# First stage of a graph and expert kernel: two node chunks with each edge group, eight places of edge coefficients, PSUM of the radial weights released at its last read

## The reference

```python
edge_index = jnp.stack([src, dst])
x = x + _L0_gnn_ref(_layernorm(x, axis=-1), edge_attr_3, edge_attr_8, L0_gnn_fc_w1, ...)

def _L0_gnn_ref(node_features, edge_vectors, edge_lengths_embedding, fc_w1, fc_w2, lin_w0, lin_w1, edge_index):
    sender, receiver = (edge_index[0], edge_index[1])
    ...
    sh1 = jnp.sqrt(3.0) * edge_vectors / (r + 1e-09)
    h = jax.nn.silu(edge_lengths_embedding @ fc_w1 / np.sqrt(NB))
    w = (h @ fc_w2 / np.sqrt(NH)).reshape(-1, NPATH, MUL)
    s = node_features[:, :MUL][sender]
    v = node_features[:, MUL:].reshape(-1, MUL, 3)[sender]
    dot = jnp.einsum('eui,ei->eu', v, sh1)
    crs = jnp.cross(v, sh1[:, None, :])
    m0 = (w[:, 0] * s + w[:, 3] * dot * inv_sqrt3) * inv_sqrt2
    m1 = (w[:, 1] * s * sh1 + w[:, 2] * v + w[:, 4] * crs * inv_sqrt2) * inv_sqrt3
    agg0 = jax.ops.segment_sum(m0, receiver, num_segments=NN) / AVG_NEIGH
    ...
    out0 = agg0 @ lin_w0 / np.sqrt(MUL)
    ...
    return upd + node_features
```

## Time and profile before

| | us |
|---|---|
| median of 3 runs | 1482.0 |
| profiled execution | 1486.56 |
| its span | 1484.8 |
| first stage, to the loads of the next | 389.4 |
| busy in the first 372 us: VectorE, GpSimd, ScalarE, TensorE | 314.0, 276.7, 273.3, 243.7 |
| mean granted TensorE clock in the first 372 us | 0.84 |

### The profile page before, as it was taken

The page is one execution under the profiler, slowest core; times in us unless marked ns, Lnnn a source line. Parts: engine busy times, 40 slices in busy tenths (PEclk is TensorE's granted clock), DMA queues, the critical chain, the costliest instruction groups (busy, mean ns, idle before and its releaser), DMA issues.

```text
span 1484.8 us, 26582 instructions
## 1 busy us (share of the span) xinstructions
PE 1223.6 (82%) x7872; PEld 1081.4 (73%) x7872; DVE 1015.4 (68%) x2130; ACT 932.9 (63%) x2049; POOL 1009.8 (68%) x915
## 2 busy tenths in 40 slices
PE   2335598998489523799999999999999999999993
PEld 0223365555355322799999999999999999999993
DVE  7889969996389897565755755665755575556653
ACT  4788967874257500666766766766766576667762
POOL 6886777875457302576777777777777777778785
PEclk9966788988799756899999999999999999999997
DMA  9999845543676101242433433343522343233333
GB/s 322 294 336 318 260 89 73 74 66 43 143 267 217 57 9 36 72 103 43 100 57 48 107 46 46 48 102 47 113 47 43 47 107 49 44 47 54 54 50 43
DMA packets 131625, 152.97 MB, mean 103 GB/s; under 512 B 17034, under 2 KB 118474, under 8 KB 131422
## 3 DMA queue, kind: packets, MB, share of 16 engines
q0 software_dynamic: 51456, 64.07, 27.4%
q1 hardware_dynamic: 58446, 66.59, 13.8%
q10 hardware_dynamic: 21648, 21.45, 4.2%
HBM read 98.79 MB, written 53.28 MB: 102 GB/s over the span
## 4 chain that ended last, share of the span: by engine, by line
PE 51%; issue 4%; POOL 2%; ACT 2%; DMA 1%; DVE 0%; ACTq 0%; POOLq 0%; DVEq 0%
PE f_ps_y L1533 25%; PE f_ps_h L1521 24%; PE f_ps_x L1511 2%; POOL out L1412 1%; POOL xg L1394 1%; POOL sg L1398 1%; ACT h_all L1461 0%; ACT h_hi L1460 0%; ACT f_xn L1445 0%; DMA sg<-stat_rows,idx_row 0%; DMA sg<-stat_rows,idx_now 0%; ACT y_all L1471 0%; DMA out<-clean,put_now 0%; ACT w_hi L1288 0%; DVE clean L1598 0%
## 5 line engine op out<-in xcount | busy, mean ns | idle before, releaser
L1460 ACT ACTIVATE h_hi<-f_ps_h,c_b 128x384 fp32r<-128x384 f32 (+1 forms) x416 | 237.0, 570 | 263.3 <-PE f_ps_h L1521 263.3
L1571 DVE TENSOR_TENSOR h_lo<-h_all,h_hi 128x768 fp32r<-128x768 f32 (+1 forms) x208 | 184.4, 886 | 257.5 <-ACT h_all L1461 257.1
L1533 PE MATMUL f_ps_y<-w_hi,h_hi 128*128 128x256 f32 x1136 | 325.1, 286 | 0.7 <-DVE h_lo L1571 0.7
L1533 PE MATMUL f_ps_y<-w_lo,h_hi 128*128 128x256 f32 x1136 | 319.8, 282 | 0.0
L1533 PE MATMUL f_ps_y<-w_hi,h_lo 128*128 128x256 f32 x1136 | 319.6, 281 | 0.0
L1412 POOL DMA_INDIRECT out<-clean,put_now x159 | 260.6, 1639 | 57.5 <-issue 49.3
L1394 POOL DMA_INDIRECT xg<-out,idx_now x159 | 193.1, 1214 | 130.8 <-issue 120.6
L1521 PE MATMUL f_ps_h<-x_hi,w_hi 128*128 128x384 f32 (+1 forms) x832 | 271.9, 327 | 7.9 <-issue 3.5
L1521 PE MATMUL f_ps_h<-x_lo,w_hi 128*128 128x384 f32 (+1 forms) x832 | 269.3, 324 | 0.0
L1521 PE MATMUL f_ps_h<-x_hi,w_lo 128*128 128x384 f32 (+1 forms) x832 | 269.0, 323 | 0.0
L1461 ACT ACTIVATE h_all<-f_ps_h,c_b 128x384 f32<-128x384 f32 (+1 forms) x416 | 237.9, 572 | 0.0
(11 more groups left out here) (214 smaller groups left out, 2285.9 us busy)
## 6 DMA issues: line engine op xcount, KB each, us to landing
shared<-out SPq DMA_DIRECT2D x40, 512.0 KB, 4.0
w_raw<-in_w SPq DMA_DIRECT2D x16, 1024.0 KB, 5.3
xin<-in_x SPq DMA_DIRECT2D x24, 512.0 KB, 8.0
out<-xin ACTq DMA_DIRECT2D x24, 512.0 KB, 7.2
shared<-in_x SPq DMA_DIRECT2D x16, 512.0 KB, 6.5
out<-shared ACTq DMA_DIRECT2D x16, 512.0 KB, 6.1
dst_row<-in_dst SPq DMA_DIRECT2D x20, 256.0 KB, 3.7
xg<-out,idx_now POOLq DMA_INDIRECT x159
```

The source lines that it names most:

```text
L1460: nc.scalar.activation(h_hi[:, f, :n * P], ps_h[:, f % SLOTS, :n * P], ACT.Relu, bias=b1[:, e, f:f + 1])
L1533: ins = nc.tensor.matmul(ps_y[:, i], x[:, f, i * P:(i + 1) * P], weights[s][:, w], start=i != 1 and f == 0 and n == 0, stop=f == KF - 1 an ...
L1571: tt(h_lo[:, pair, :n * P], h_all[j % 2][:, :, :n * P], h_hi[:, pair, :n * P].bitcast(F32), ALU.subtract).then_inc(h_lo_ready, 1)
```

## The change

Steps with two chunks: `STEPS` goes from 5 to 10, and each of VectorE's steps 0 to 7 has two chunks, one inside the messages and one behind them. Chunk coefficients are taken behind the messages. Edge statistics and coefficients have eight places (`AHEAD = 8`) and are spread by two small functions. On ScalarE the hidden layer of group g+1 comes ahead of its rows, the aggregate's copy between the two halves of the directions. On GpSimd each pair of gathers stands ahead of a batch's scales, with one or two edge scales behind; one batch fewer is done there (`BY_POOL` 7); the late gathers stand behind scatters 5, 6 and 7, edge scales seven groups ahead from scatter 3 on. SP loads the receivers' rows inside the loop over chunks. In the messages the last product that reads `ps_w` comes earlier and has a semaphore of its own, `w_taken`, on which TensorE's next radial weights wait. The line numbers of the changed kernel are a few higher up to the middle of the stage and lower after it (L402 becomes L399, L481 L479, L604 L601, L717 L715).

```diff
-    STEPS = 5
+    STEPS = 10
+    AHEAD = 8
-    BY_POOL = 8
-    assert NC == 4 * STEPS
+    BY_POOL = 7
+    assert NC == 2 * STEPS
...
-        edge_mv = [sb(f"edge_mv{h}", [P, GT, 2]) for h in range(4)]
+        edge_mv = [sb(f"edge_mv{h}", [P, GT, 2]) for h in range(AHEAD)]
...
@@ SP
-                if c % 4 == 1:
-                    next_embedding(c // 4)
-                    if c > 4:
-                        next_receivers(c // 4 - 1)
+                if c % 2:
+                    next_embedding(c // 2)
+                    if c > 2:
+                        next_receivers(c // 2 - 1)
...
@@ GpSimd
             for n in range(3, BY_POOL):
+                gather(2 * n - 1)
+                gather(2 * n)
                 node_scales(n)
-                for g in (2 * n - 1, 2 * n):
-                    if g < SLOTS:
-                        gather(g)
-                if n % 2:
-                    edge_scales(n // 2 + 2)
+                edge_scales(2 * n - 3)
+                if 2 * n - 2 < STEPS:
+                    edge_scales(2 * n - 2)
+            gather(2 * BY_POOL - 1)
             pool.wait_ge(chunks_known, 16)
             for g in range(EG):
                 scatter(g)
-                if STEPS <= g + 4 < EG - 1:
-                    edge_scales(g + 5)
-                if 1 <= g < 4:
-                    gather(SLOTS + 2 * g - 2)
-                    gather(SLOTS + 2 * g - 1)
+                if STEPS <= g + 7 < EG:
+                    edge_scales(g + 7)
+                if 5 <= g < 8:
+                    gather(SLOTS + 2 * (g - 5))
+                    gather(SLOTS + 2 * (g - 5) + 1)
...
@@ ScalarE
             for g in range(1, STEPS):
-                c = 4 * g
-                add_own_rows(c)
-                take_agg(g - 1)
-                radial_hidden(g + 1)
-                next_rows(g + 1)
-                add_own_rows(c + 1)
-                rows_by_direction(g + 1, (0, 1))
-                take_upd(g - 1)
-                add_own_rows(c + 2)
-                rows_by_direction(g + 1, (2, 3))
-                add_own_rows(c + 3)
-            store_rows(NC - 1, 1)
+                add_own_rows(2 * g)
+                radial_hidden(g + 1)
+                if g + 1 == STEPS:
+                    add_own_rows(2 * g + 1)
+                    store_rows(NC - 1, 1)
+                next_rows(g + 1)
+                rows_by_direction(g + 1, (0, 1))
+                take_agg(g - 1)
+                if g + 1 < STEPS:
+                    add_own_rows(2 * g + 1)
+                rows_by_direction(g + 1, (2, 3))
+                take_upd(g - 1)
             for g in range(STEPS, EG + 1):
                 if g + 1 < EG:
+                    radial_hidden(g + 1)
                     next_rows(g + 1)
-                    rows_by_direction(g + 1, range(GT))
+                    rows_by_direction(g + 1, (0, 1))
                 take_agg(g - 1)
                 if g + 1 < EG:
-                    radial_hidden(g + 1)
+                    rows_by_direction(g + 1, (2, 3))
                 take_upd(g - 1)
...
@@ TensorE, radial_second
-                    pe.wait_ge(msg_ready, g)
+                    pe.wait_ge(w_taken, g)
...
@@ VectorE
                 chain.mark(tt(tmp_d[:], tmp_f[:], w(3), ALU.mult))
+                chain.wait(1)
+                tt(vec(tmp_h), vec(tmp_a), w3(4), ALU.mult).then_inc(w_taken, 1)
                 chain.mark(tt(tmp_g[:], tmp_b[:], tmp_c[:], ALU.add))
-                chain.wait(2)
-                chain.mark(tt(vec(tmp_h), vec(tmp_a), w3(4), ALU.mult))
...
             def step(g):
                 receivers(g)
-                if g + 1 < STEPS:
-                    node_coefs(BATCH[4 * g + 2])
-                    node_statistics(4 * g + 4)
-                    messages(g, 4 * g + 5)
-                    edge_statistics(g + 3)
-                    node_coefs(BATCH[4 * g + 4])
-                    edge_coefs(g + 2)
-                    node_statistics(4 * g + 6)
-                    node_statistics(4 * g + 7)
+                if g + 2 < STEPS:
+                    messages(g, 2 * g + 4)
+                    node_coefs(BATCH[2 * g + 2])
+                    node_statistics(2 * g + 5)
                 else:
-                    if g + 1 == STEPS:
+                    if g + 2 == STEPS:
                         node_coefs(BATCH[NC - 1])
                     messages(g)
-                    edge_statistics(g + 3)
-                    edge_coefs(g + 2)
+                for n in range(EG):
+                    if statistics_step(n) == g:
+                        edge_statistics(n)
+                for n in range(EG):
+                    if coefs_step(n) == g:
+                        edge_coefs(n)
+            def statistics_step(n):
+                return (n - 3) // 2 if n < STEPS else n - 6
+            def coefs_step(n):
+                if n < 2:
+                    return -1
+                return (n - 1) // 2 if n < STEPS else n - 2
```

More of the change, by code:

```diff
@@ L264, in edge_and_node_block @@
         msg_ready = sem("msg_ready")
+        w_taken = sem("w_taken")
         row_ready = sem("row_ready")
@@ L322, in _ @@
             for c in range(NC):
-                for a in range(2):
-                    if 1 <= c and c + RING - 1 < NC:
+                if c:
+                    for a in range(2):
                         sp.wait_ge(x1_out[(c - 1) % RING][a], 16 * ((c - 1) // RING + 1))
-                        load_rows(c + RING - 1, a)
-                if 1 <= c and c + RING - 1 < NC:
+                        if c + RING - 1 < NC:
+                            load_rows(c + RING - 1, a)
                     sp.sem_inc(stored, 1)
```

42 lines of the change are left out of this document (18 added, 24 removed).

## The result

The changed kernel takes 1546.7 us (median of 4 runs, 1543.3 to 1552.5) against 1482.5 for the kernel before on the same chip: ratio 1.044, 95% interval 1.040 to 1.048. It is 64 us slower. The forecast was 1477.0 with a range of 1469 to 1489, and none of the rivals is near it. The profiled execution took 1543.27 us with a span of 1541.5, 56.7 more than before. The first stage accounts for that: the start of its last group of scatters, S(19), goes from 379.97 to 437.96, +58.0 us.

The account below looks back on a forecast made before the run. GpSimd's chain of scatters was taken to bound the first stage, with VectorE nearly as long. Start 127.4 plus intervals of 60.0, 64.5, 90.5 and 32.6 put S(19) at 375.0, -5.0 us: 1477.0 us, range 1469 to 1489.

Parts of the forecast that it names:

- what is late next: Steps with chunks: hidden layer waits for TensorE's aggregate, delaying the receivers' row; 1 to 2 us lost a step.
- the rest of the new order: Remaining reordering, with VectorE's leftover waits and extra 2.5 us: hidden by 24 us of slack, so no cost.
- the last eleven intervals: Last scatter intervals on GpSimd: eight of 11.31 us, then three of 10.86 with VectorE done; 123.1 us.
- S(0): Start of the first group's first scatter on GpSimd: 127.4, 3.0 us late; bounds 126.5 and 130.4.
- VectorE in the chunk steps: Steps 0 to 2 on VectorE, with two chunks each: 20.15 us a step.
- Waits for the receivers' row: VectorE's new wait: 2 us a step up to step 3, some 6 us more in steps 4 and 5.
- Five intervals beside traffic: First five scatter intervals, beside the chunks' transfers: 12.0 us each, 60.0 in all; ends 11.31 and 14.35.
- rival A: First five scatter intervals: beside chunk traffic each stays at 14.35 us, +6.8 us, 1489; chance 0.20.
- Three intervals with gathers: Scatters 5, 6 and 7 on GpSimd, eight gathers behind each: 21.5 us an interval, 64.5 in all.
- VectorE's wait for the weights goes: VectorE's waits for radial weights in PSUM fall from 18.0 us to under 3 through earlier release and hidden layer.
- The bound: First stage's end: set by GpSimd's chain of scatters at 375.0; VectorE's 336 and its 15.0 us path give 351.
- The falsifier written down: End of the first stage: argument wrong if last scatters wait for ScalarE's update, or S(19) comes before 360.

Follow-up runs that it names:

- the middle order: Changed kernel with ScalarE's loop without chunks reordered: next rows, two directions, aggregate's copy, hidden layer, other directions; ratios 1.0026 and 1.0023 against the kernel before.

## Why the prediction was wrong

**The step that failed** is the one that asked what is late next: "The hidden layer now needs TensorE to be through with the aggregate of two groups back, and ScalarE's next rows stand behind it". That named two links of the loop, and I priced them where the trace had a second consumer, the receivers' row in the steps with chunks. I never followed the sentence round in the steps with edges alone: rows, directions, copy of the aggregate, transform, radial weights, aggregate, first radial matmul, hidden layer. In the sum this stood at nothing: "the rest of the new order" was left to 24 us of slack, and the last eleven intervals went in at the pace of the landings, 123.1 us. The durations were in the trace of the kernel before. ScalarE's "about 6 us" stands in the prediction, and TensorE has near 300 us:

```profile
299.13 3.39 PE L572 MATMUL ps_agg<-lin,agg 128*128 128x128 f32 x16 [1.46 <-ACT agg L492]
302.44 2.68 PE L553 MATMUL ps_w<-fc,hidden 64*128 64x320 f32 x8
305.05 4.61 PE L564 MATMUL ps_agg<-same,msg 128*128 128x512 f32 x16
309.59 1.07 PE L546 MATMUL ps_h<-emb,fc 8*64 8x512 f32 x2
```

From start to start that is 6.1 + 3.3 + 2.6 + 4.5 + 1.1 = 17.6, against the 11.31 of the chain from the earlier trace rows: 10 groups of +6.3 us, 63, against the 58.3 that were found. With the weights and the aggregate of the earlier trace rows, 4.60 and 7.26 us, it comes to 22.4, the length of a long period; but the rows alone did not say where the slow matmuls would fall. Putting the order back (S(19) 380.6), putting it into the kernel before (+85 us) and taking one link out (11.53 a group) show it. VectorE's last message ended at 423.3, where 336 was taken, so there was no slack either.

**S(0)**: 127.4 taken, 125.39 measured, inside the bounds, 2.0 us too late. **VectorE in the chunk steps**: step length 20.15 taken; steps 0 to 2 took 20.0 to 20.2, and steps 3 and 4, which are shorter, 18.5 and 18.8. Waits for the receivers' row 12.0 us in four, where 8 were taken. Right in kind and nearly in size, but not in place: there is none up to step 4, 3.1 us lie ahead of steps 5 and 6 and 8.9 us ahead of steps 9 and 10.

**Five intervals beside traffic**: 60 taken, 67.7 measured in this profile, 65.4 over six. This term was mis-sized by 5 to 8 us and is rival A's mechanism at 13.1 us an interval, between my 12.0 and its 14.35. The Trainium skill says in "DMA: Bandwidth & Descriptors", section "SWDGE vs HWDGE vs iDMA", that GpSimd's ring and the hardware queues' rings take turns in a DMA engine. By that rule scatters beside more traffic are dearer, and the traces have this sign: 13.1 us at about 250 GB/s, 11.9 at 185, the latter in one profile. With the start, the traffic and the gathers as measured and no loop the sum is 375.0 - 2.0 + 5.4 - 1.0 = 377.4, and the last eleven intervals took 124.7 to 125.9 us with the loop open where 123.1 were taken: 379 to 380, the value of before. So the forecast gain of 5 us was not there even without the loop; the three profiles with ScalarE's loop open have 376.1, 380.6 and 385.2.

**Three intervals with gathers**: 64.5 taken, 63.5 measured. **The last eleven**: 123.1 taken, 181.4 measured: the loop, +58.3. The sum: -2.0 + 7.7 - 1.0 + 58.3 = +63.0 on 375.0, which is 438.0.

**VectorE's wait for the weights goes**: it grew to 80.9 us. The release is not what it waited for (18.5 us with the release alone). With the middle order it falls to between 0 and 10.8 us, where under 3 was forecast, and with the loop open in the old order it is 18.5: it follows the copy of the aggregate. **The bound**: that the scatters, not VectorE, set the stage's end would have been right without the loop (S(19) falls to 360 with half of them, in the middle order); in the changed kernel it was wrong. The path behind VectorE's last message is 10.6 and not 15.0 us. That message ends at 352.1 and 355.6 with the middle order, where 336 was taken; its waits for rows and weights come to 20.4 and 25.2 us, where 8 were taken.

The falsifier written down, "the last scatters wait for ScalarE's update", is what happened, from S(10) to S(18). What was missing is a rival for it: an order changed on ScalarE deserved one.

## What to carry to other kernels

When an instruction is moved ahead of others on an in-order engine, follow all that now stands behind its wait through the other engines until it ends or comes back; if it comes back, add the durations once round and compare the sum with the present bound of an iteration, for every loop of the program and the steps with the least other work above all. In the waits such a loop shows as a circle of engines that wait for each other, none of them busy all the time, at a steady period. An idle stretch is worth filling only where nothing else sets the next start, which a run with half the work of the supposed bound shows.

## What was not expected of the hardware

In the loop two periods of 17.8 us are followed by one of 22.2, in three profiles of two kernels, each of another group of runs, with a granted TensorE clock of 0.70 in the long and 0.71 to 0.81 in the short; the same aggregate takes 6.78 and 4.61 us. In the periods from 307 to 378 us the clock is at 0.50 to 0.54 over the transform behind the 6.1 us of idle, where 0.50 is half of full speed; in the long one it is 0.50 over the radial weights too and 0.66 over the aggregate. Over the last ten groups the mean granted clock was 0.75 in the changed kernel and 0.93 and 0.86 in the two profiles of the middle order; in the first of these TensorE's waits for the aggregate's copy from 300 to 345 us are 0.7 us in four. In these traces a loop of waits costs twice, in TensorE's pauses and in slower matmuls behind them. Why every third period is the long one is not shown.

The kernel before had medians of 1482 to 1546 us in five groups of runs. In the two profiles at hand, with spans of 1484.8 and 1524.2 us, the start of its last scatters differs by 0.9 us; the difference lies in the last two stages. And one kernel's S(19) differed by 9 us between two executions (middle order) and by 7 (changed kernel), so single profiles of a stage that runs beside traffic don't carry a claim of a few us.
